# Five more edge steps fetched row by row, by DMAs that ScalarE issues

## What is computed

```python
x_src = x[src]
x_dst = x[dst]
theta_x = (x_dst - x_src) @ theta_w.T + theta_b
phi_x = x_src @ phi_w.T + phi_b
e = jax.nn.relu(theta_x + phi_x)
out = jax.ops.segment_max(e, dst, num_segments=x.shape[0])
out = jnp.where(jnp.isfinite(out), out, 0.0)
x = _layernorm(x + out, axis=-1)
```

## Time and profile before

| | |
|---|---|
| median of 3 runs | 1034.67 us (1034.25 to 1035.08) |
| the profiled execution | 1036.28 us |
| its span, first to last instruction | 1034.5 us |
| POOL busy | 771.0 us |
| PE busy, matmuls | 837.8 us |
| DVE busy | 693.0 us |
| ACT busy | 336.8 us |
| PEclk, share of TensorE's full clock granted | 0.923 over the span |

### The profile page before, as it was taken

How to read it: one execution, slowest core, us unless ns; L and a number is a source line. 1 busy time by engine, 2 the same in 40 slices (tenths; PEclk the granted TensorE clock), 3 DMA queues, 4 the chain that set the end, 5 groups by cost and what they waited for, 6 DMA issues and landing times. The chain is left out here.

```text
span 1034.5 us, 15863 instructions
## 1 busy us (share of the span) xinstructions
PE 837.8 (81%) x3875; PEld 437.8 (42%) x3875; DVE 693.0 (67%) x1732; ACT 336.8 (33%) x701; POOL 771.0 (75%) x793
## 2 busy tenths in 40 slices
PE   5976899999999999999999999999998946650000
PEld 5832444445444544454445444454443335440000
DVE  6734666766767767676766767767765546565698
ACT  3921233333333333233333333333221121110366
POOL 6877777777777777777777777777777777775773
PEclk9988999999999999999999999999998969885555
DMA  8955667687777777767777777777866789974365
GB/s 273 368 179 179 219 221 238 220 267 228 240 243 239 248 233 240 250 221 254 236 243 241 245 240 239 231 253 233 263 221 223 231 276 311 283 239 161 117 203 177
DMA packets 116641, 243.80 MB, mean 236 GB/s; under 512 B 19632, under 2 KB 57733, under 8 KB 116549
## 3 DMA queue, kind: packets, MB, share of 16 engines
q1 hardware_dynamic: 78244, 138.69, 37.5%
q0 software_dynamic: 37728, 103.04, 34.7%
q10 hardware_dynamic: 576, 1.06, 0.3%
HBM read 127.29 MB, written 115.45 MB: 235 GB/s over the span
## 5 line engine op out<-in xcount | busy, mean ns | idle before, releaser
L465 POOL DMA_INDIRECT rows<-b_table,idx x684 | 660.6, 966 | 208.5 <-issue 176.2
L639 PE MATMUL ps_a<-work,shared 128*128 128x512 bf16 x2940 | 667.1, 382 | 37.8 <-DVE work L819 37.0
L639 PEld LDWEIGHTS ps_a<-work,shared 128*128 128x128 bf16 x2940 | 281.3, 98 | 386.2 <-DVE work L819 47.7
L549 ACT COPY hist<-acc 128x512 f32<-128x512 f32 x253 | 148.7, 588 | 489.2 <-DVE hist L863 488.9
L863 DVE SCALAR_TENSOR_TENSOR acc<-hist,reset,rows 128x256 f32<-128x256 f32 x154 | 76.1, 494 | 195.3 <-issue 157.3
L819 DVE TENSOR_SCALAR work<-batch,node 128x512 bf16<-128x512 int16 x490 | 161.5, 373 | 6.2 <-PE ps_a L639 6.2
L863 DVE SCALAR_TENSOR_TENSOR acc<-acc,reset,rows 128x256 f32<-128x256 f32 x253 | 124.7, 493 | 49.4 <-DMA rows<-b_table,idx 36.8
L863 DVE SCALAR_TENSOR_TENSOR hist<-acc,reset,rows 128x256 f32<-128x256 f32 x253 | 122.3, 484 | 27.3 <-DVE acc L863 1.8
L700 PE MATMUL ps_a<-theta_sb,shared 128*128 128x256 f32 x196 | 56.9, 446 | 36.2 <-DVE shared L909 27.5
L451 POOL DMA_INDIRECT early<-in_x,idx_first x51 | 58.7, 1150 | 17.7 <-issue 15.2
L700 PEld LDWEIGHTS ps_a<-theta_sb,shared 128*128 128x128 f32 x196 | 41.7, 223 | 51.4 <-issue 44.7
(11 more groups left out here) (129 smaller groups left out, 481.2 us busy)
## 6 DMA issues: line engine op xcount, KB each, us to landing
runmax<-hist SPq DMA_DIRECT2D x260, 384.0 KB, 3.1
direct<-b_table SPq DMA_DIRECT2D x896, 1.0 KB
rows<-b_table,idx POOLq DMA_INDIRECT x684, 3.5
b_table<-rows SPq DMA_DIRECT2D x7, 896.0 KB, 7.4
shared<-in_xt SPq DMA_DIRECT2D x49, 128.0 KB, 4.4
early<-in_x SPq DMA_DIRECT2D x12, 512.0 KB
out<-hist SPq DMA_DIRECT2D x11, 512.0 KB, 3.3
hist<-in_xt SPq DMA_DIRECT2D x7, 512.0 KB, 7.9
```

Of the source, the lines that this page charges most:

```text
L465: pool.indirect_dma_start(out=rows[:, PLACE[k], :], out_offset=None, in_=b_table, in_offset=bass.IndirectOffsetOnAxis(ap=idx[:, k:k + 1], ...
L549: nc.scalar.copy(hist[:, slot:slot + n - 1, :], acc[:, at:at + n - 1, :]).then_inc(s_copied, 1)
L639: mm = pe.matmul(ps_a[banks(b)[k]][:].rearrange("p j d -> p (j d)"), split[:, part, t, k * P:(k + 1) * P], hot[:, i % HOT, :], start=(t == ...
```

## The change

Five more steps leave POOL: the first steps of groups 47, 91, 133, 175 and 221 (`ACT_GROUPS`). Their 640 rows are fetched by ACT with DMAs of a single row, three a group behind the copy of maxima, from group 0 to 213; the numbers come from a new small tensor `idx_act`, by loads of 16 registers. The rows land in three buffers that are otherwise idle until the end: `late_max`, `scanned` and `fix`, in turn. Therefore the clearing of these three moves from the start to behind group 221 on DVE (the clearing of `fix`/`none` at the start stays), POOL waits for it (`s_cleared`) ahead of its fetch into `fix`, and ACT waits before its first group for the table, the numbers and the written empty row. Before a buffer's second use ACT waits for the fold that read it. A fold of such a step waits until its 128 rows have landed.

```diff
+ACT_GROUPS = (47, 91, 133, 175, 221)
+ACT_ROWS = 3
+ACT_LOADED = 16
+    CLEAR_AT = ACT_GROUPS[-1]
-    GATHERED = [k for k in range(STEPS) if k not in EARLY_OF and k not in PRODUCT_OF and k not in DIRECT_OF]
+    GATHERED = [k for k in range(STEPS) if k not in EARLY_OF and k not in PRODUCT_OF and k not in DIRECT_OF
+                and k not in ACT_OF]
+        by_act = [late_max[:], scanned[:].rearrange("p k n -> p (k n)")[:, 0:D], fix[:]]
-            pool.wait_ge(s_idx, 16)
+            pool.wait_ge(s_idx, 32)
+            pool.wait_ge(s_cleared, 3)
             act.dma_start(idx[:], src).then_inc(s_idx, 16)
+            act.dma_start(idx_act[:], src_act).then_inc(s_idx, 16)
+            act.wait_ge(s_idx, 32)
+            act.wait_ge(s_bout[0], 16 * (CHUNKS + 1) // 2)
+            act.wait_ge(s_bout[1], 16 * (CHUNKS // 2))
+            act.wait_ge(s_noneout, 16)
+            def load_row(i):
+                m, p = divmod(i, P)
+                if p == 0 and m >= len(by_act):
+                    act.wait_ge(s_fold, ACT_STEPS[m - len(by_act)] + 1)
+                if p % ACT_LOADED == 0:
+                    held["rows"] = nc.values_load_multi_w_load_instructions(
+                        idx_act[i // ACT_LOADED:i // ACT_LOADED + 1, :], engines=[mybir.EngineType.Activation], min_val=0,
+                        max_val=N - 1, skip_runtime_bounds_check_because="src holds row numbers of x")[1]
+                act.dma_start(by_act[m % len(by_act)][p:p + 1, :],
+                              b_table[bass.ds(held["rows"][p % ACT_LOADED], 1), :]).then_inc(s_by_act[m], 16)
                 nc.scalar.copy(hist[:, slot:slot + n - 1, :], acc[:, at:at + n - 1, :]).then_inc(s_copied, 1)
 
+                for i in range(ACT_ROWS * g, min(ACT_ROWS * (g + 1), len(ACT_STEPS) * P)):
+                    load_row(i)
-            nc.vector.memset(late_max[:], -FLT_MAX)
-            nc.vector.memset(scanned[:, :, 0:1], 0.0)
+                if START[g] in ACT_OF:
+                    dve.wait_ge(s_by_act[ACT_OF[START[g]]], 16 * P)
+                if g == CLEAR_AT:
+                    dve.wait_ge(s_fold, STOP[g])
+                    nc.vector.memset(late_max[:], -FLT_MAX).then_inc(s_cleared, 1)
+                    nc.vector.memset(scanned[:, :, 0:1], 0.0).then_inc(s_cleared, 1)
+                    nc.vector.memset(fix[:], -FLT_MAX).then_inc(s_cleared, 1)
```

More of the change, by code:

```diff
@@ L34, with build @@
 A_ROUND = 2
-def build(nc, x, xt, src_first, src_direct, src, src_t, dst, theta_t, phi_t, theta_b, phi_b, out):
+def build(nc, x, xt, src_first, src_direct, src_act, src, src_t, dst, theta_t, phi_t, theta_b, phi_b, out):
     N, D = x.shape
@@ L94, in build @@
     DIRECT_STEPS = list(DIRECT_OF)
+    ACT_OF = {START[g]: m for m, g in enumerate(ACT_GROUPS)}
+    ACT_STEPS = list(ACT_OF)
+    assert all(k not in EARLY_OF and k not in PRODUCT_OF and k not in DIRECT_OF for k in ACT_STEPS)
+    assert all(ACT_ROWS * (g - 3) >= P * (m + 1) for m, g in enumerate(ACT_GROUPS)) and P % ACT_LOADED == 0
+    CLEAR_AT = ACT_GROUPS[-1]
     assert all(k not in EARLY_OF and k not in PRODUCT_OF for k in DIRECT_STEPS) and DIRECT_STEPS[-1] < START[NG - 8]
@@ L110, in build @@
     LATE_STEPS = STEPS - KEPT
-    assert ENDS_AT < LATE
+    assert ENDS_AT < LATE and CLEAR_AT < LATE
     assert (NT - 1) % X_TILES == 0 and EMPTIED < NG and max(X_AT) < NG
     assert ENDS_AT < NG and max(A_AT) < NG and max(CONVERTED_AT) < LATE and max(SIGN_AT) < EDGES_AT
-    GATHERED = [k for k in range(STEPS) if k not in EARLY_OF and k not in PRODUCT_OF and k not in DIRECT_OF]
+    GATHERED = [k for k in range(STEPS) if k not in EARLY_OF and k not in PRODUCT_OF and k not in DIRECT_OF
+                and k not in ACT_OF]
     PLACE = {k: i % SLOTS for i, k in enumerate(GATHERED)}
@@ L192, in build @@
         idx_direct = sb("idx_direct", [DIRECT * P // LOADED, LOADED], I32)
+        idx_act = sb("idx_act", [len(ACT_GROUPS) * P // ACT_LOADED, ACT_LOADED], I32)
         idx_first = sb("idx_first", [P, EARLY], I32)
@@ L283, in build @@
         s_rownums = sem("row_numbers_loaded")
+        s_cleared = sem("fix_rows_cleared")
+        s_by_act = [sem(f"rows_loaded_by_act{m}") for m in range(len(ACT_GROUPS))]
         s_direct = [sem(f"rows_loaded_one_by_one{m}") for m in range(DIRECT)]
@@ L532, in _ @@
             act.wait_ge(s_xrows, 16 * EARLY)
+            act.wait_ge(s_idx, 32)
+            act.wait_ge(s_bout[0], 16 * (CHUNKS + 1) // 2)
+            act.wait_ge(s_bout[1], 16 * (CHUNKS // 2))
+            act.wait_ge(s_noneout, 16)
+            held = {}
+            def load_row(i):
[8 more added lines that the diff above has]
+                              b_table[bass.ds(held["rows"][p % ACT_LOADED], 1), :]).then_inc(s_by_act[m], 16)
             for g in range(NG):
@@ L827, in row_at @@
                     return far[:, PRODUCT_OF[k][1], :]
+                if k in ACT_OF:
+                    return by_act[ACT_OF[k] % len(by_act)]
                 if k in DIRECT_OF:
@@ L979, in _ @@
             scales(len(TAIL) - 1, deviations(len(TAIL) - 1))
-_INS = ["x", "xt", "src_first", "src_direct", "src", "src_t", "dst", "theta_t", "phi_t", "theta_b", "phi_b"]
+_INS = ["x", "xt", "src_first", "src_direct", "src_act", "src", "src_t", "dst", "theta_t", "phi_t", "theta_b", "phi_b"]
 def kernel(x, src, dst, L0_gnn_theta_w, L0_gnn_theta_b, L0_gnn_phi_w, L0_gnn_phi_b):
@@ L1008 @@
         "src_first": by_p.reshape(P, steps)[:, [GROUP * g for g in EARLY_GROUPS]],
+        "src_act": by_p.reshape(P, steps).T[[GROUP * g for g in ACT_GROUPS]].reshape(-1, ACT_LOADED),
         "src_direct": by_p.reshape(P, steps).T[[GROUP * g for g in DIRECT_GROUPS]].reshape(-1, LOADED), "dst": windows,
```

## The result

The kernel after takes 1024.47 us (median of 4 runs, 1023.29 to 1026.35) against 1034.46 of before beside it: a ratio of 0.9907, 95% interval 0.9889 to 0.9926. The profiled execution has a span of 1022.9 us.

A forecast was written before the change was run, and what follows sets the result against it. GpSimd (POOL), issuing 684 table gathers back to back, was taken as the bound. Five gathers fewer gave -6.35 us, all other terms nothing: 1034.67 - 6.35 = 1028.3 us, range 1026.3 to 1034.5, its own 1026.5 to 1030.1.

The forecast's parts named there:

- own range: Whole kernel: 1026.5 to 1030.1 us around the forecast, chance 67%, allowing the last gather's landing to be 1.8 us off.
- POOL's string: GpSimd's 684 table gathers, issued one after the other, set the end: 869.1 us with idle, 1.271 us a gather.
- Part 1: GpSimd's table gathers: five fewer at 1.271 us each, -6.35 us, with the end merely moved earlier.
- Part 2: ScalarE's 640 single-row DMAs: 0.39 us each, three a group 1.17 us, nothing counted for copies in flight hiding issues.
- Part 3: ScalarE's 40 loads of 16 numbers: 2.2 us each (1.5 to 2.9), 0.41 us a group.
- Cover: ScalarE's idle time hides rows and loads: 2.69 of 3.23 us a group used; nothing put down for lateness.
- Part 4: Small accompanying edits: start load, ScalarE's new waits, moved DVE memsets, POOL's wait; no cost or gain, sum stays -6.35.
- (a): DMA engines: single rows burden one engine, gathers land late; about 1059 us at 0.35 us a row; 3%.
- (c): ScalarE: a row costs over 0.57 us and makes it the bound; 1176 us at 0.8 us; 4%.
- (d): At the end: part of the gain lost through a later last landing or DVE behind; 1031 us; 6%.
- (b): ScalarE's lateness delays DVE, TensorE stands; +54 us, 1082; sign: DVE's copy waits; 9% slower, 11% gain lost.
- slack of 14 us: DVE's folds against POOL's ring of gather slots: DVE may fall 14 us later before POOL feels it, an estimate.

The follow-up runs named there:

- e2: The changed kernel, unaltered, measured and traced again: 1026.98 us, ratio 0.9928 to before.
- e3: Changed kernel without its 640 row DMAs and 40 number loads; the five steps' folds read a constant tile: 1027.84 us, ratio 0.9932 to before.
- e8: Changed kernel with a second single-row DMA of 32 numbers behind each row, six issues a group: 1025.73 us, ratio 0.9926 to before.
- e4: Only the accompanying edits (load of numbers, moved memsets, waits); GpSimd keeps 684 gathers, ScalarE fetches no row: 1032.69 us, ratio 0.9981 to before.
- e5: Changed kernel with all 640 ScalarE rows and also all 684 GpSimd gathers, whose rows the folds read: 1033.01 us, ratio 0.9995 to before.
- e1: The kernel of before, unaltered, measured and traced again: 1034.25 us, ratio 1.0009.
- e6: Changed kernel with DVE's third bf16 parts made for 8 of 256 columns only, the rest cleared once: 1022.21 us, ratio 0.9891 to before.
- e16: The changed kernel on another chip, where before takes 1373.81 us: 1395.91 us, ratio 1.0186.
- e7: Changed kernel with four rows a group and seven steps on ScalarE, 677 gathers left: 1023.96 us, ratio 0.9912 to before.
- e11: As e3, but with the first load of numbers and first 12 row DMAs, where before takes 1374.18 us: 1361.61 us, ratio 0.9891.
- e15: As e3, but with the first load of numbers and first 12 row DMAs, where before takes 1373.81 us: 1365.32 us, ratio 0.9959.
- e10: Changed kernel with DVE's 1.2 us rest and third-part operations in four cuts, where before takes 1374.18 us: 1401.14 us, ratio 1.0201.

## Why the prediction missed

The forecast named the mechanism rightly and the gain too small; the first measurement also lies at the favourable edge of what repeats. The four measurements with 679 gathers and DVE's work as in after (after, e2, e3, e8) have 0.9907, 0.9928, 0.9932 and 0.9926: a mean of 0.9923, 7.9 us. That would be 1026.5 us, on the lower edge of my own range; the 2.1 us more of the first measurement are luck.

- **Bound, POOL's string: right.** 679 gathers, every gap 0.3 us or less.
- **Part 1, -6.35: right.** By pairs 4.9 us (e4 to e3) and 6.9 (e5 to e2). The table strings with 684 gathers average 868.3 us over four traces (before, e1, e4, e5), those with 679 861.9 over five (after, e2, e3, e6, e8): 6.4.
- **Part 2, 0.39 a row: right**, 0.39 from one start to the next in the plain case (1.02 with the last issue counted to its end). "I count nothing for that" left out that the issues run beside the copy.
- **Part 3, 2.2 us a load: too dear.** The hole is 1.57 us in the rows above and 1.8 on average. The estimate of 1.8 by the floor that the Trainium skill gives ("DMA: Bandwidth & Descriptors", Latency and other measured facts) was nearer.
- **Cover: right on this chip.** ScalarE's idle time fell by 110 us of 600. I expected less than half of 287 to be left, and 176.8 are: the room was larger than the sum said, because of the overlap.
- **Part 4, "Sum: -6.35", the term 0 for the edits that come along: this is the step that failed**, and with it Part 1's "the end behind POOL's string is the same work, moved earlier". e4 puts these edits at -2.0 us (0.5 to 3.5): with -6.35 that makes -8.4, near the mean of 7.9. As far as the traces tell, they act at the end and not at the start: from the last gather to the write of the repaired rows it takes 7.6 to 8.4 us in the eight traces with them and 9.6 in the two without, 1.2 to 2.0 us less. e5, with the same edits and all rows, is only 0.5 us under before (0.6 over to 1.8 under), so the size lies between 0.5 and 2 us and is not settled; why the edits shorten the end stays open.
- **The rest of the first trace, the start 3.00 us earlier and 1.25 us less stretching**, is not these edits: e4 starts at 78.36 us as before does. "Nothing there moves" fails only in the kernels with rows, by 1 to 3 us, and part of it is which gathers meet a DVE operation.
- **Own range 1026.5 to 1030.1: too narrow, and for the reason given with it.** I let only the last landing vary. It moved by 1.22 us, within the 1.8 allowed, but I had given it no direction; the long gathers, 1.8 us instead of 0.95, which the mean of 1.271 against the plain 1.25 had shown, have a width of their own that I gave nothing: what the table's gathers took above 0.945 us each is 11.5 to 15.8 us over the ten traces up to e8, and the 51 gathers took 71.7 to 74.5 us in nine of them (70.25 in e6). Single runs of before range over 1031.3 to 1039.3 in 23 runs beside e1 to e4.
- **Rivals.** (a) and (c) did not occur: no gather waits, and a row costs 0.39. (d) did not either. (b), ScalarE's lateness, is refuted here by e2 against e3 and by e8. On the other chip on which after ran, where the slack of 14 us does not exist, the kernel is 22 us slower (e16) beside a priced +54, but not by the sign that I gave for (b): DVE's waits for ScalarE's copies do not grow, those for SP's stores do.

What stays open: why POOL's first table gather comes at 75.6 to 77.1 us in all traces with the 640 rows (after, e2, e5, e7, e8) and at 78.1 to 78.8 in those without (before, e1, e3, e4), although the rows come later than that start (e6, with rows and small third parts, has 74.10); and why e5's time shows so little of it. The first landing differs with it, 3.8 to 4.1 us against 4.3 to 4.6, but e11 and e15, with 12 rows, have 3.81 and 3.80.

## What to carry to other kernels

Where POOL's issuing of gathers sets the end, single rows fetched by the queues of engines with idle time are a net gain, priced at the removed gathers (1.25 us each here), as long as the engine can take them behind a wait. Price the edits that come along by a kernel of their own, and give a term that is "unchanged" the width by which its pieces differ between two traces of one kernel. Slack holds for the chip that was profiled: on one where POOL had to wait for folds, the same change cost 1.9% instead of giving 0.8%.

## What the runs showed of the hardware

- ScalarE issues DMAs while its own copy runs: the first row's issue begins 0.13 us into a copy of 0.59 us, three rows are through in 1.02 us, and with six issues a group the kernel is no slower (0.9926).
- POOL's indirect gather of 128 rows takes 0.95 us, and 1.7 to 1.9 when it begins 0.1 to 0.35 us behind the start of a DVE operation of 1.22 us on 128x1024; beside one of 0.19 us it takes 0.94. All 85 gathers of x over 1.5 us end 0.81 to 0.83 us behind the end of a DVE operation, and cut into four such an operation lets the gather go earlier (1.17 us in e10).
- The Trainium skill ("DMA: Bandwidth & Descriptors", Issuing engines are not separate DMA queues) says that issuing from several engines saves only the sequencer's time to start a DMA, usually small beside the DMA. The first half agrees; small it is not here, where POOL's 679 gathers with the idle time before each, 861.6 us, are 84% of the span.
- 640 single-row DMAs more made no gather wait for a fold longer than 0.3 us, and the 1280 of e8 did not either.
- On a chip on which before takes 1374 us the ratio of the change is 1.0186, and four row issues by SP can take up to 11.0 us instead of 1.5. A second such chip (1370 us) ran only the kernels with nine steps and with quarters, at 1.0236 and 1.0216.
